# A state-space layer and two attention layers on one core: first and last elements specialised, norm shifts moved to GpSimd, the order written in three parts

## The reference

```python
# block 1: selective state space, D_INNER = 256, D_STATE = 16
xz = x @ in_proj_w; xb, z = split(xz)
xb = silu(causal_conv4(xb))
proj = xb @ x_proj_w
dt = softplus(proj[..., :8] @ dt_proj_w + dt_proj_b); b, c = proj[..., 8:24], proj[..., 24:]
state = exp(dt * a) * state + dt * b * xb        # for each token in order
y = (sum_s state * c + D_param * xb) * silu(z)
return y @ out_proj_w
# block 2: DEPTH = 2 layers: shift, qkv, l2-normalised q and k with rotary tables,
# local attention (8 heads, window 64), residual; shift, norm, gated MLP (341), residual
```

## Time and profile before

| | |
|---|---|
| median of 3 runs | 2419.76 us (2418.8 to 2420.0) |
| profiled execution | 2425.17 us, span of its instructions 2423.4 us |
| busy: PE, DVE, ACT, POOL | 1934.9, 1914.2, 1741.6, 1716.1 us |
| mean granted TensorE clock | 0.934 of 2.4 GHz |

### The profile page before, as it was taken

One profiled execution on the slowest core, in us unless ns is written; L12 is line 12 of the kernel. 1 busy time (PEld: TensorE's weight loads), 2 busy tenths in 40 slices (PEclk: granted clock), 3 DMA queues, 4 the chain that ended last, 5 costly groups with the idle time before them and its releaser, 6 DMA issues.

```text
span 2423.4 us, 43963 instructions
## 1 busy us (share of the span) xinstructions
PE 1934.9 (80%) x15823; PEld 1138.6 (47%) x15936; DVE 1914.2 (79%) x3509; ACT 1741.6 (72%) x3891; POOL 1716.1 (71%) x1572
## 2 busy tenths in 40 slices
PE   2255889798988979797988979797988979788866
PEld 0012446363635446363645546363644536364634
DVE  3557797979889797988888797988889797987442
ACT  2245778696978778696877879696877869686644
POOL 1959596877959596886959596895959597792110
PEclk9967999998999999899999989999999999899988
DMA  5444343535345453535434353534434353541000
GB/s 167 126 114 119 107 119 96 131 101 145 100 118 131 107 123 89 142 82 151 113 110 122 108 125 95 142 91 132 124 105 119 106 133 94 140 104 34 17 16 14
DMA packets 126346, 261.09 MB, mean 108 GB/s; under 512 B 26928, under 2 KB 59696, under 8 KB 125872
## 3 DMA queue, kind: packets, MB, share of 16 engines
q1 hardware_dynamic: 126128, 258.27, 40.4%
HBM read 185.42 MB, written 42.99 MB: 94 GB/s over the span
## 4 chain that ended last, share of the span: by engine, by line
PE 37%; ACT 18%; DVE 18%; POOL 14%; issue 10%; DMA 2%; SPq 0%; POOLq 0%; DVEq 0%; ACTq 0%
POOL dbu L663 5%; POOL gy L680 5%; ACT late L893 4%; DVE m L928 4%; PE b_bank L357 3%; PE f_bank L357 3%; ACT da L609 3%; DVE kr L942 3%; PE b_bank L763 2%; POOL kr L997 2%; PE y_sum L584 2%; PE b_bank L780 2%; PE b_bank L746 2%; PE f_bank L746 2%; PE f_bank L763 2%
## 5 line engine op out<-in xcount | busy, mean ns | idle before, releaser
L629 DVE TENSOR_TENSOR_SCAN hs<-da,dbu 128x512 f32<-128x512 f32 x512 | 623.3, 1217 | 112.5 <-POOL dbu L663 67.6
L680 POOL TENSOR_TENSOR gy<-hs,bc 128x512 f32<-128x512 f32 x512 | 652.7, 1275 | 34.2 <-DVE hs L629 21.8
L663 POOL TENSOR_TENSOR dbu<-spread,bc 128x512 f32<-128x512 f32 x512 | 652.2, 1274 | 16.5 <-DMA spread<-steps 16.5
L609 ACT ACTIVATE da<-spread,rest 128x512 f32<-128x512 f32 x512 | 362.3, 708 | 140.2 <-DVE hs L629 121.1
L720 PE MATMUL b_bank<-rest,h_t 128*128 128x512 f32 x384 | 245.8, 743 | 75.4 <-DVE kr L942 71.5
L997 POOL TENSOR_TENSOR kr<-kr,rn 128x512 f32<-128x512 f32 x256 | 261.0, 1044 | 32.9 <-ACT rn L853 18.4
L720 PE MATMUL f_bank<-rest,h_t 128*128 128x512 f32 x384 | 235.8, 717 | 40.2 <-DVE kr L942 30.4
L584 PE MATMUL y_sum<-gy,rest 128*32 128x512 f32 x1024 | 146.4, 647 | 93.3 <-POOL gy L680 93.3
L357 PE MATMUL b_bank<-first,kr 128*128 128x128 f32 x768 | 127.5, 291 | 82.3 <-DVE kr L942 60.4
L893 ACT ACTIVATE late<-b_bank,mx 128x128 f32<-128x128 f32 x512 | 141.0, 383 | 60.5 <-DVE mx L958 60.5
L1146 POOL TENSOR_TENSOR xs<-xs,v 128x512 f32<-128x512 f32 x16 | 18.9, 1183 | 215.9 <-ACT xs L352 215.9
(11 more groups left out here) (171 smaller groups left out, 4789.3 us busy)
## 6 DMA issues: line engine op xcount, KB each, us to landing
spread<-steps SPq DMA_DIRECT2D x256, 512.0 KB, 4.7
vs<-v SPq DMA_DIRECT2D x96, 260.0 KB, 5.6
steps<-k_t SPq DMA_DIRECT2D x32, 512.0 KB, 3.0
bc<-bc_rows SPq DMA_DIRECT2D x32, 512.0 KB, 6.4
gate<-gates SPq DMA_DIRECT2D x32, 512.0 KB, 5.4
gates<-kr SPq DMA_DIRECT2D x16, 512.0 KB, 2.9
gates<-late SPq DMA_DIRECT2D x16, 512.0 KB, 3.9
vs<-v SPq DMA_DIRECT2D x32, 130.0 KB, 4.7
```

The source lines that it names most:

```text
L609: e.activation(da[:, :], spread[:, slot(b, s // 2), 0, :], ACT.Exp, scale=a_neg[:, s:s + 1]).then_inc(decayed.sem, 1)
L629: e.tensor_tensor_scan(hs[:, s % 2, :], da[:, :], dbu[:, s % 2, :], 0.0, ALU.mult, ALU.add).then_inc(scanned.sem, 1)
L663: e.tensor_tensor(dbu[:, s % 2, :], spread[:, slot(b, s // 2), 1, :], bc[:, s % 2, :], ALU.mult).then_inc(fed.sem, 1)
L680: e.tensor_tensor(gy[:, s % 8, :], hs[:, s % 2, :], bc[:, 2 + s % 2, :], ALU.mult).then_inc(read_out.sem, 1)
```

## The change

Nothing of what is computed changes. (1) For element 0 the entry uses seven banks (`entry_bank`), since no other stream uses them yet, and VectorE, not GpSimd, makes dt and dt*u. (2) In states 0 and 1 the read-out is shared (`by_dve`): VectorE does two of three products in state 0, one of three in state 1; and the decay alternates between `da` and `lb[0]`, for which layer 1 of element 0 waits for the last scan of state 1. (3) Layer 1 of element 15 uses all eight banks (`bank_list`, `head_banks`), with `gy` and `bc` as more room for squares and rotated q, and its heads' steps are written so that two pairs are open at once. (4) The shifts of `n_x` and `n_o` are made by GpSimd (`pool_shift`), and `n_x` is applied by ScalarE. (5) `ORDER` has three words for each engine, a first, one that is repeated eleven times, and a last. The first covers elements 0 to 3 of E; the last holds nearly the words of before for the run-out.

```diff
+ROUNDS = 11
...
-def weave(word, late, **chains):
+def weave(first, usual, last, **chains):
...
+    for word in (first, *[usual] * ROUNDS, last):
...
+            def bank_list(self, b):
+
+                if self is wb and b == B - 1:
+                    return [*lb, da, y_sum, *fa]
+                return self.banks
+
+            def head_banks(self, b):
+
+                L = self.bank_list(b)
+                if len(L) == 3:
+                    return [L[0:2]] * 4, [L[2]] * 8
+                return [L[0:2], L[3:5]] * 2, [L[2], L[5]] * 4
...
+        def pool_shift(E, e, w, b, negated, shifted):
+            E.wait_ge(*w.measured(b, 1))
+            e.tensor_scalar(w.mr[:, :], w.mv[:, :, 0], -1.0, None, ALU.mult).then_inc(negated.sem, 1)
+            E.wait_ge(*w.scaled(b, 1))
+            E.wait_ge(*negated(b))
+            e.tensor_tensor(w.mr[:, :], w.mr[:, :], w.rs[:, :], ALU.mult).then_inc(shifted.sem, 1)
...
+        def entry_bank(b, part):
+
+            if b:
+                return e_bank
+            return dict(turn=e_bank, i0=fa[0], i1=fa[1], i2=fa[2], i3=lb[0], x=lb[1], d0=fa[0], d1=fa[1])[part]
...
-                E.wait_ge(*before)
-                e.matmul(e_bank[:, :], w_in[:, i * P:(i + 1) * P], xn_t, start=True, stop=True).then_inc(in_projected.sem, 1)
-                yield
-            E.wait_ge(*z_made(b, 1))
+                E.wait_ge(*(before if b else e_copied(0)))
+                e.matmul(entry_bank(b, f"i{i}")[:, :], w_in[:, i * P:(i + 1) * P], xn_t, start=True, stop=True).then_inc(in_projected.sem, 1)
+                yield
+            E.wait_ge(*(z_made(b, 1) if b else u_made(0, 1)))
...
+                if b == 0 and h == NH2 - 1:
+                    for _ in step_inputs(E, e, 0):
+                        pass
...
+        def by_dve(b, s):
+
+            return b < SHARED and (s % 3 > 0, s % 3 == 1,)[b]
...
+        def decay(b, s):
+
+            return lb[0] if b < 2 and s % 2 else da
...
+            act_normalise(E, e, n_x, b, lambda t: xs[b % 3][:, t, :], lambda t: x1[:, t, :]).then_inc(x2_made.sem, 1)
...
+                if s > 1 and by_dve(b, s - 2):
+                    E.wait_ge(*reads(b, s - 2)[-1])
                 E.wait_ge(*decayed(b, s))
                 E.wait_ge(*fed(b, s))
-                e.tensor_tensor_scan(hs[:, s % 2, :], da[:, :], dbu[:, s % 2, :], 0.0, ALU.mult,
+                e.tensor_tensor_scan(hs[:, s % 2, :], decay(b, s)[:, :], dbu[:, s % 2, :], 0.0, ALU.mult,
                                      ALU.add).then_inc(scanned.sem, 1)
+                if s and by_dve(b, s - 1):
+                    read_product(E, e, b, s - 1)
+                if s == NSCAN - 1 and by_dve(b, s):
+                    read_product(E, e, b, s)
...
-            E.wait_ge(*n_x.scaled(b, 1))
-            if b > 2:
-                E.wait_ge(*stored(b - 3))
-            for t in range(NT):
-                op = e.tensor_scalar(xs[b % 3][:, t, :], x1[:, t, :], n_x.mv[:, t, 0:1], n_x.rs[:, t:t + 1], ALU.subtract,
-                                     ALU.mult)
-            op.then_inc(x2_made.sem, 1)
...
+                if not by_dve(b, s):
+                    read_product(E, e, b, s)
...
+                if bank is lb[0] and n == 2 and b == 0:
+                    E.wait_ge(*scanned(1, NSCAN - 1))
...
+            if wide:
+                score(1)
+                yield
+                for g in range(HEADS // 2):
+                    for hd in (2 * g, 2 * g + 1):
+                        turn(hd)
+                        yield
+                    for hd in (2 * g, 2 * g + 1):
+                        value(hd)
+                        yield
+                    if g < 2:
+                        score(g + 2)
+                        yield
+                    else:
+                        turn_out(g - 2)
+                        yield
+            for g in range(0 if wide else HEADS // 2):
                 turn(2 * g)
...
+            pool_shift(E, e, n_x, b, x_negated, x_shifted)
+            yield
...
-            dve_norm_shift(E, e, n_o, b)
...
```

More of the change, by code:

```diff
@@ L93, in use_table @@
             self.e.preload_act_table_set(name)
-def weave(word, late, **chains):
-    late = {part[0]: int(part[1:]) for part in late.split()}
-    while chains:
+def weave(first, usual, last, **chains):
+    for word in (first, *[usual] * ROUNDS, last):
         for part in word.split():
             for _ in range(int(part[1:])):
[L102 to L105, removed]
+                next(chains[part[0]])
+    for chain in chains.values():
+        for _ in chain:
+            raise AssertionError("a step is left over")
 def build(nc, a, out):
@@ L411, in dve_enter @@
             for h in range(NH2):
+                bank = entry_bank(b, f"i{h}")
                 E.wait_ge(*pad_zeroed(b))
@@ L436, in pool_steps @@
                 yield
+        def pool_steps(E, e, b):
+            if b:
+                yield from step_inputs(E, e, b)
+            else:
+                for _ in range(2 * NH2):
+                    yield
         def pe_enter(E, e, b):
@@ L508, in act_steps, with reads, read_product @@
             yield
+        SHARED = 2
+        def by_dve(b, s):
+            return b < SHARED and (s % 3 > 0, s % 3 == 1,)[b]
+        def reads(b, s):
+            if b >= SHARED:
+                return [read_out(b - SHARED, s)]
+            n = [0, 0]
+            for other in range(b + 1):
+                for step in range(s + 1 if other == b else NSCAN):
+                    n[by_dve(other, step)] += 1
+            return [sem(k - 1) for sem, k in ((pool_read, n[0]), (dve_read, n[1])) if k]
+        def read_product(E, e, b, s):
+            E.wait_ge(*c_loaded(b))
+            E.wait_ge(*scanned(b, s))
+            if s > 7:
+                E.wait_ge(*summed_up(b, 2 * (s // 8 - 1) + s % 2))
+            elif b > 0:
+                E.wait_ge(*x1_made(b - 1))
+            e.tensor_tensor(gy[:, s % 8, :], hs[:, s % 2, :], bc[:, 2 + s % 2, :], ALU.mult).then_inc(
+                (read_out if b >= SHARED else dve_read if by_dve(b, s) else pool_read).sem, 1)
         def group_rows(b, g):
@@ L542, in sp_state @@
             if b > 0:
-                E.wait_ge(*read_out(b - 1, NSCAN - 1))
+                for done in reads(b - 1, NSCAN - 1):
+                    E.wait_ge(*done)
             load_bc(1, c_loaded)
@@ L581, in pe_state @@
                     E.wait_ge(*skipped(b - 1, 1))
-                E.wait_ge(*read_out(b, 8 * (m // 2) + 6 + k))
+                for done in reads(b, 8 * (m // 2) + 6 + k):
+                    E.wait_ge(*done)
                 for j in range(4):
@@ L705, in pe_attention @@
         def pe_attention(E, e, b, w, l, x, f):
+            L = w.bank_list(b)
+            wide = len(L) > 3
             for n, take in enumerate(TAKES):
-                kind, t, bank = take[0], int(take[1]), w.banks[(n + 1) % 3]
-                if n > 2:
-                    E.wait_ge(*w.freed(b, TAKES[n - 3]))
-                elif b > 0:
+                kind, t, bank = take[0], int(take[1]), L[(n + 1) % len(L)]
+                if n >= len(L):
+                    E.wait_ge(*w.freed(b, TAKES[n - len(L)]))
+                elif b > 0 and bank in w.banks:
                     E.wait_ge(*(f.added(b - 1) if bank is f.sum else f.gated(b - 1, 2)))
@@ L881, in act_attention, with weigh @@
                     yield
-            X = w.banks[0:2]
-            for hd in range(HEADS):
+            XS, _ = w.head_banks(b)
+            def weigh(hd):
+                X = XS[hd // 2]
                 E.wait_ge(*w.peaked(b, hd))
@@ L969, in share @@
                 yield
+            if len(L) > 3:
+                for hd in range(2):
+                    peak(hd)
+                    yield
             for hd in range(0, HEADS, 2):
-                peak(hd)
-                yield
-                peak(hd + 1)
-                yield
+                for other in range(hd, hd + 2) if len(L) == 3 else range(hd + 2, min(hd + 4, HEADS)):
+                    peak(other)
+                    yield
                 if hd:
```

154 lines of the change are left out of this document (86 added, 68 removed), and 72 rows, old and new, of the table ORDER.

## The result

The changed kernel takes 2386.29 us (median of four runs, 2373.24 to 2392.03) against 2419.88: ratio 0.9843, 95% interval 0.9812 to 0.9874. It is faster by 34 us; I had said 58. The measured time lies inside the stated range (2333 to 2392), but 24 us above the predicted 2362 and outside the 2350 to 2376 to which I gave 0.60. The profiled execution is its slowest run (2392.03 us, span 2390.2), 33.1 us under that of before.

What follows compares the result with a forecast made beforehand. No engine was full; GpSimd's two multiplications per scan set the pace wherever scans run. Terms of -11, -13, -7, +1, -10 and -18 (-58) gave 2367 profiled, 2362 at the median; forecast 2350 to 2376, range 2333 to 2392.

Steps and rivals of the forecast that it cites:

- The middle: -10 us over 12.5 turns: Middle elements: norm work leaves VectorE, scan-stretch work unchanged; -0.8 us a turn, ends -2 and +0.8, together -10 us.
- norm part: Middle turns: first norm to ScalarE, shifts to GpSimd; rows gave 0.2 to 0.5 us a turn, taken as 0.8.
- The prediction named this: Stated main way to be wrong: an unseen wait in the reordered middle, each us costing 12.5 us of the sum.
- Entry: Before the first scan: separate banks and VectorE's dt and dt*u bring that scan from 56.4 to 45.1 us, -11 us.
- State 0: Element 0's state 0: shared read-out, GpSimd held by VectorE's products, 2.44 to 2.05 us a step, -13 us.
- Rival B: States 0 and 1: VectorE and GpSimd do not hold each other, -24 and -13 us, total 2345; chance 0.08.
- State 1 and first layer: Element 0: a third of state 1's read-outs shared, -7 us; first layer starts later behind its norm, +1 us.
- Last layer: Last element's second layer in eight banks: projections -9.7 us, heads and output 34.7 to 26.4, together -18 us.
- Rival C: Start gives half, 15 of 30 us, and the last layer 12 as its steps wait: 2383; chance 0.15.
- A: Middle gives much more, VectorE's 3.1 us coming off each turn: 2333; chance 0.12.
- D: Middle's first layers start late, ScalarE's norm waiting for a shift behind GpSimd's step products: 2425; chance 0.05.

Runs made afterwards that it cites:

- hybrid1: Changed kernel's operations, banks and waits; its order only up to the first step of state 1, then before's order with moved norm steps: 2369.14 us.
- vector_norm: Changed kernel, but VectorE again applies the first norm and makes the output norm's shift, at before's places in the changed order: 2425.0 us, ratio 1.0007.
- pool_reads: Changed kernel, but GpSimd makes all read-out products in states 0 and 1; the second decay tile stays: 2406.13 us, ratio 0.9938.
- narrow_last: Changed kernel, but the last element's second layer stays in three banks: 2406.04 us, ratio 0.9942.
- warm: Changed kernel plus some 29 extra unread TensorE products a turn, after the layers' projections and transposes: 2409.97 us.

## Why the prediction was right, and where it was not

By place, from the profiled executions (my term; changed kernel; hybrid1):

| | predicted | changed | hybrid1 |
|---|---|---|---|
| first scan | -11 | -13.7 | -13.2 |
| state 0's 32 scans | -13 | -11.7 | -11.4 |
| from there to element 1's first layer | -6 | -2.3 | -4.1 |
| middle, to the last element's second layer | -10 | +10.2 | -15.1 |
| last layer | -18 | -15.6 | -14.9 |
| all | -58 | -33.1 | -58.8 |

The last layer is counted from its first `h_t` (2322.57 us before, 2305.06 after). The columns compare single executions: those of before and of the changed kernel are the slowest of their runs, hybrid1's is its fastest. At the median hybrid1 gains 51 us (2420.4 to 2369.14), so its agreement with -58 in this table is in part luck of the execution.

**The step that failed** is "The middle: -10 us over 12.5 turns". Its norm part came out: alone, in before's order, it gave 9.6. That was half luck, since my rows gave 0.2 to 0.5 a turn, I took 0.8 without a reason from them, and most of the 0.75 measured came from fewer turns of 139 us. But I costed the new order at nothing ("in the scan stretch its work is unchanged"), and it costs 11 to 17 us at the median (changed kernel against hybrid1, by ratios or by medians), and 25 in the profiled middle. Of these 25, 20 stand in turns 1 to 13, 10 of them in turns 1 and 2, which the order's first part writes. The scan stretch, which I had held to be unchanged, takes 94.8 to 102.2 us for 97, and the time behind it is 41.7 us where it is 39.6 in before's order with the same operations. The prediction named this as what would make it wrong. I had read the order's pieces for what stands where, and not for how much slack is left when TensorE's products take longer. In the long turn a scan waits for its decay where the short one does not (first the long turn, then the same scan of the short one):

```profile
703.36 1.22 DVE L770 TENSOR_TENSOR_SCAN hs<-da,dbu 128x512 f32<-128x512 f32 x1 [1.02 <-ACT da L744]
```

```profile
1256.42 1.23 DVE L770 TENSOR_TENSOR_SCAN hs<-da,dbu 128x512 f32<-128x512 f32 x1
```

Which engine's rows of the new order cause it was not tried one by one, and stays open; the wait for the output projection is where I would look first. Why the changed kernel finds the short turns after some elements, and vector_norm never, is open too.

**Entry.** Right to 3 us. The order of the chain was as worked out, and the chain ended earlier: the second Abs at 25.3 us, where I had 29.1, since the projection to steps took 1.91 us for my 3.6, and the two step projections 1.98 for 4.1. The two products ahead of them that the chain needs were hardly faster than worked out. VectorE's dt and du then ended at 30.8 for 34.7. The tables became the last wait, held by GpSimd: a term that I had not weighed.

**State 0.** Size nearly right: 2.15 us a step where I had 2.05, and 2.52 before where I had 2.44. Of the 11.7 us the share gave 9.9 (pool_reads); the rest came with the order and the second decay tile. The mechanism was half right. The read-out products of VectorE (21 in state 0, 11 in state 1), and GpSimd's products there:

```profile
L636 DVE TENSOR_TENSOR gy<-hs,bc x32: 660/666/1745, 47.8 to 229.8; 128x512 f32<-128x512 f32 x32
```

```profile
L800 POOL TENSOR_TENSOR dbu<-spread,bc 128x512 f32<-128x512 f32 x30 | 41.0, 1381 | 1.7 <-DVE hs L770 1.7
...
L636 POOL TENSOR_TENSOR gy<-hs,bc 128x512 f32<-128x512 f32 x11 | 16.8, 1528 | 7.5 <-DVE hs L770 5.4 <-PE y_sum L713 2.2
```

I had expected VectorE's well over 0.69: their median is 0.666, and in state 0 only two of the 21 took over 0.7 (in state 1 six of the 11, up to 1.53). It is mostly GpSimd that is held, 1.38 and 1.53 us on average for the 1.26 of the earlier trace rows. Here the product of VectorE starts first and GpSimd's takes longer, then the other way round:

```profile
47.78 0.67 DVE L636 TENSOR_TENSOR gy<-hs,bc 128x512 f32<-128x512 f32 x1
48.01 1.56 POOL L800 TENSOR_TENSOR dbu<-spread,bc 128x512 f32<-128x512 f32 x1 [0.25 <-DVE hs L770]
```

```profile
85.69 1.26 POOL L800 TENSOR_TENSOR dbu<-spread,bc 128x512 f32<-128x512 f32 x1
85.75 1.75 DVE L636 TENSOR_TENSOR gy<-hs,bc 128x512 f32<-128x512 f32 x1
```

A held product cost GpSimd some 0.3 to 0.5 us and not my 0.55. The step is no shorter for it, because GpSimd now waits: it is busy for 58.95 of 67.8 us, where it was for 77.32 of 79.5. So two errors of the working nearly cancel. Rival B (1.68 a step) is excluded. The Trainium skill, "SBUF — State Buffer", section "Who interferes with whom", has the shared pair of ports as an exclusive lock, held for the whole instruction by the engine that issues first. Both pairs of rows agree with it, and so do the tables' 4.90 us beside GpSimd's products.

**State 1 and first layer.** -6 expected, -2.3 measured: state 1's scans take 85.1 us for 91.6 (-6.5), but 34.2 for 32.3 pass ahead of them and 23.4 for 21.1 behind them (+4.2). The share there is worth 5 (pool_reads). Element 0's first layer, whose norm now comes later, starts 22.0 us after the last scan and not 19.2; I had worked out 3.5 for this and held all but 1 hidden behind state 1's loads; now GpSimd goes from a head product of that layer (142.16 us) straight to state 1's first feed (143.16).

**Last layer.** Projections to 0.2 us; heads 28.6 for 26.4, mis-sized by 2.2. The banks alone were worth 15.2 (narrow_last).

**Rivals.** Rival C's number, 2383, is nearest to the result, but its mechanism is not what happened: the start gave 28 of 30 and the last layer 15.6. A and B fall with the rows above. D fails by its size, and its place is excluded: in the changed kernel ScalarE's pieces of the first norm wait for GpSimd's shift three times in all, for 3.2 us together.

## What to carry to other kernels

Cost a reordered steady state by itself, with the old order and the new edits as a run of its own; here the edits gave 51 us and their new order took back 11 to 17. Where a loop's length repeats to 0.1 us, look at all its turns and at more than one profile: the changed kernel had two lengths, and a single turn's rows show one. An order written for the ends should hand over to the proven one as soon as the ends' own work is issued; here that gave 2369.14 us, against 2375.69 with the proven order throughout, a small step (the intervals of the ratios overlap).

## What was not expected of the hardware

The distance between turns stays at 136.5 us for five elements and at 139.9 us for eight, to 0.1 us, and moves between such values within two or three elements. The mean clock did not tell fast from slow: hybrid1 ran at 0.922 to 0.928 and took 2369.14 us, the changed kernel at 0.933 to 0.944 and took 2386.29, warm at 0.952 to 0.957 and took 2409.97. In the entry the granted clock does not tell how fast the products go: it is 1.00 from 8 to 25 us, but the pieces of its 512-column products start 0.85 to 1.01 us apart up to 14.7 us and 0.43 to 0.54 from 15.4 on, within each run of them; in the kernel before they start 0.85 to 1.03 apart in all of element 0's entry, at 1.00 too. In state 0 the clock then fell to a mean of 0.53, against 0.93 before, at no visible cost: the sum's products, too, come 0.85 us apart in both kernels (at 57.6 and 58.4 us here with the clock at 0.50, at 75.4 and 76.2 before with it at 1.00), and TensorE is busy for 15.81 us here and 15.94 before.
